# One-core Trainium2 kernel, linear attention, two mixtures of experts and a gated scan: late weights requested earlier, expert choice split over scan steps, state copies moved to ScalarE, last scan step in halves

## The chip, the cores and the metric

The kernel runs on one core of a Trainium2 chip. The metric is the device time of one execution in microseconds (us); three executions of the kernel before were timed, and one more was profiled.

## The reference, cut to what matters

The input is one sequence of 4096 rows of 256 numbers. All is float32.

```python
xn = layernorm(x)
x = x + chunk_attention(xn) + sum_e sigmoid(xn @ sel[e]) * (relu(xn @ keys[e]) @ values[e])   # 16 experts, dense
xn = layernorm(x)
g, v, d = (xn @ W[m] + b[m] for W, b in the three weights)        # m in 0..3
h[m] = scan over rows: h_t = a_t * h_(t-1) + sigmoid(g) * tanh(v),  a = 0.001 + 0.998 * sigmoid(d)
x = x + sum_m comb[:, m] * h[m]                                    # comb: softmax of the top 2 of 4 gates
      + w2[e] @ relu(w1[e] @ xn + b1[e]) + b2[e],  e = argmax of 8 # one expert for a row
```

## The kernel before, in words

Rows are worked in 8 groups of 512 rows (4 tiles of 128). Every float32 product is three matmuls of rounded parts (high x high, high x low, low x high, helper `mm3`, L374 on); so each operand has to be split in a high part (ScalarE) and a low part (VectorE) first.

**Stage A** (to about 522 us) does the attention and the dense experts of all groups. At its end SyncE's queue stores the gate mixture of the first 24 tiles (`mixture_store`, L525) and waits for that store (L693) before it goes on.

**Scan groups 0 to 3** (522 to 664 us). A group is 8 steps, step i for gate m = i // 2 and half c = i % 2 of the channels. TensorE makes three products of 512 columns (`scan_products`, L535) into three PSUM banks, ScalarE applies sigmoid, tanh and sigmoid and makes `a_b` (L1444), VectorE multiplies `xs_b` (L1697; GpSimd does it in group 0, L1549), scans (L1703), copies the last column to `hstate` (L1706), and multiplies by the mixture `comb_b` (L1714). From step 2 on the result is added to `accO` or `accT`, by GpSimd (`mix`, L1552) or by VectorE (L1723) where `mixed_on_dve(g)` holds: groups 2, 3 and 7. TensorE turns `accT` back to rows (`to_rows`, L1325) in step 2 of the next group as a rule. TensorE reuses a PSUM bank two steps later, ScalarE its output buffer two steps later. The six split weights of gates 2 and 3 (`WB_late`) come by six loads of 512 KB (`load_late`, L1180), the mixture of a group by a broadcast load of 1 MB (`load_comb`, L1159), the transposed rows of a group by two loads of 512 KB (`load_x1T`, L1150). For group 1 that load comes behind a wait (L1203) for the gate logits of the last group, which VectorE reads in group 0, step 5.

Within group 0, TensorE still turns and gates the last group's rows: it needs the low part `nT_l` (VectorE, L419, in front of step 3) for the gate matmuls (L459), whose result VectorE reads after step 5 (L435). Behind that, `choose_expert` (L1619) finds the expert of all 32 tiles in six operations on 128x256. The counts of rows per expert, the row positions and the table of expert slots follow in groups 1 and 2, and GpSimd scatters the rows to their experts' blocks.

**Experts** (664 to 903 us): 23 slots, of 256 rows or of 128 (every third). A slot is a first product (w1), relu and split, then a second product (w2). The halves of w1 and w2 are split ahead. In the first slot both ScalarE and VectorE split the second half of w2 (`w2_half(n, 1)`, L1492 and L1791) before they touch the first relu. SyncE's queue is one list written by hand: in `slot` (L1267) it waits until a half of w2 is split before it loads the next into its place, and behind that wait stand the biases b2, the rows, the small w1 and the bias b1 of the next slot (`load_b1`, L1244), which ScalarE's first relu of that slot needs.

**Scan groups 4 to 7** (903 us to the end). GpSimd gathers each row's expert result (`gather`, L1576) into `y_b` one group at a time, after the last use of the buffer, and gathers those of groups 0 to 2 between; GpSimd also adds the mixture in groups 4 to 6. In `total` (L1725) VectorE adds `y_b` to `x1_b` (L1735) and the turned scan result (L1744, for the last group L1741 in two pieces), and SyncE stores the sum before it loads the next `x1_b`. After the last step the chain is: xs, scan, copy, mixture, addition, four transposes (L1334), two sums (L1741), two stores (L1319).

```python
step(0, i)                      # VectorE, group 0 (L1813 to L1816)
if i == 5:
    gate_logits(dve, g)
    choose_expert()
```

## Time and profile before

| | |
|---|---|
| timed runs | 1053.69, 1055.35, 1055.56 us; median 1055.35 |
| the profiled execution | 1056.41 us, its span 1054.6 us |
| mean granted TensorE clock | 0.996 of full speed |
| TensorE (PE) busy | 1029.5 us, 98% |
| VectorE (DVE), ScalarE (ACT), GpSimd (POOL) busy | 753.7, 626.4, 366.9 us |

The span runs from the first to the last instruction; the remaining 1.8 us lie around it. In the rows, L with a number is a line of the kernel, the first number of a timeline row is the start in us from the span's start, the second the duration (of all the xN instructions that the row merges, from the first start to the last end), and square brackets give how long the engine sat idle just before and what ended that. SPq is SyncE's queue of DMA issues.

### The profile page before, as it was taken

How to read it: one execution, taken by the hardware profiler on the slowest of the kernel's cores; microseconds unless marked ns; L12 is line 12 of the kernel's file. 1: busy time of each engine (PE TensorE's matmuls, PEld its weight loads, DVE VectorE, ACT ScalarE, POOL GpSimd, SP SyncE). 2: the span in 40 equal slices, each digit the busy share in tenths (PEclk: the TensorE clock that was granted, in tenths of full speed). 3: DMA queues.
4: the chain of work that ended last, by engine and by line, in shares of the span. 5: the costliest groups of instructions: out<-in, count | busy, mean ns of one | idle time of the engine just before them, and what ended most of it. 6: DMA issues, size and time to landing. Idle time of an engine off the chain costs nothing. (4 is left out here: it accounts for less than half of the span.)

```text
span 1054.6 us, 19932 instructions
## 1 busy us (share of the span) xinstructions
PE 1029.5 (98%) x6564; PEld 920.0 (87%) x6564; DVE 753.7 (71%) x1264; ACT 626.4 (59%) x1138; POOL 366.9 (35%) x305
## 2 busy tenths in 40 slices
PE   6999999999999999999999999999999999999996
PEld 5898898989889898898877888899999999888885
DVE  4875756656575576767769879877777677488788
ACT  4553544444444454545565656788888888566664
POOL 2444453444444344343453783000000000264441
PEclk9999999999999999999999999999999999999998
DMA  5207111010111201513156266578877876332314
GB/s 162 91 17 239 41 40 60 0 64 35 40 60 40 85 15 40 181 61 140 41 202 259 93 214 243 199 241 264 273 264 249 276 249 210 126 125 100 116 58 139
DMA packets 74847, 141.07 MB, mean 134 GB/s; under 512 B 9904, under 2 KB 42544, under 8 KB 73776
## 3 DMA queue, kind: packets, MB, share of 16 engines
q1 hardware_dynamic: 65872, 126.94, 35.1%
q0 software_dynamic: 3072, 8.39, 2.4%
q10 hardware_dynamic: 5856, 5.15, 1.5%
q8 instruction: 25, 0.41, 0.2%
q14 instruction: 22, 0.18, 0.1%
HBM read 101.86 MB, written 38.60 MB: 133 GB/s over the span
## 5 line engine op out<-in xcount | busy, mean ns | idle before, releaser
L734 POOL TENSOR_TENSOR acc<-acc,ytmp 128x512 f32<-128x512 f32 x120 | 156.4, 1303 | 245.9 <-ACT ytmp L823 227.3
L1439 ACT ACTIVATE act_o<-ps,scan_bias 128x512 f32<-128x512 f32 x192 | 130.1, 688 | 106.5 <-PE ps L380 90.9
L823 ACT ACTIVATE ytmp<-ps,sel 128x256 f32<-128x256 f32 x256 | 107.6, 472 | 100.4 <-PE ps L1041 99.8
L889 DVE SCALAR_TENSOR_TENSOR hT_l<-ps,hT_h 128x512 fp32r<-128x512 f32 x128 | 87.7, 685 | 104.1 <-ACT hT_h L786 103.9
L1039 PE MATMUL ps<-vals_h,hT_h 128*128 128x256 f32 x512 | 145.2, 284 | 0.8 <-DVE hT_l L889 0.7
L1040 PE MATMUL ps<-vals_l,hT_h 128*128 128x256 f32 x512 | 143.6, 280 | 0.0
L1041 PE MATMUL ps<-vals_h,hT_l 128*128 128x256 f32 x512 | 143.5, 280 | 0.0
L786 ACT ACTIVATE hT_h<-ps 128x512 fp32r<-128x512 f32 x128 | 76.5, 598 | 96.1 <-PE ps L380 95.9
L1580 POOL DMA_INDIRECT y_b<-y_d,pos_i x20 | 25.6, 1280 | 290.0 <-DMA y_d<-y_sb 267.1
L925 DVE SCALAR_TENSOR_TENSOR acc<-ps,sel,acc 128x256 f32<-128x256 f32 x240 | 104.0, 474 | 3.0 <-PE ps L1041 2.9
L1703 DVE TENSOR_TENSOR_SCAN h_b<-a_b,hstate,xs_b 128x512 f32<-128x512 f32 x64 | 90.0, 1406 | 22.2 <-ACT a_b L1444 16.9
L378 PE MATMUL ps<-xT_h,keys_h 128*128 128x512 f32 x256 | 104.8, 409 | 0.7 <-DVE xT_l L419 0.7
L1039 PEld LDWEIGHTS ps<-vals_h,hT_h 128*128 128x128 f32 x512 | 96.3, 188 | 9.2 <-issue 2.5
L380 PE MATMUL ps<-xT_h,keys_l 128*128 128x512 f32 x256 | 101.1, 395 | 0.0
L379 PE MATMUL ps<-xT_l,keys_h 128*128 128x512 f32 x256 | 101.0, 394 | 0.0
L1040 PEld LDWEIGHTS ps<-vals_l,hT_h 128*128 128x128 f32 x512 | 96.2, 188 | 4.4
L1041 PEld LDWEIGHTS ps<-vals_h,hT_l 128*128 128x128 f32 x512 | 96.8, 189 | 0.0
L1412 PE MATMUL ps<-w_h,eT_h 128*128 128x256 f32 x312 | 90.2, 289 | 4.6 <-DVE eT_l L1765 4.0
L1413 PE MATMUL ps<-w_l,eT_h 128*128 128x256 f32 x312 | 87.9, 282 | 0.0
L1414 PE MATMUL ps<-w_h,eT_l 128*128 128x256 f32 x312 | 87.8, 281 | 0.0
L1765 DVE TENSOR_TENSOR eT_l<-t,eT_h 128x512 fp32r<-128x512 f32 (+1 forms) x92 | 55.7, 610 | 38.9 <-ACT eT_h L1488 38.7
L378 PE MATMUL ps<-x1T,WB_h 128*128 128x512 f32 (+1 forms) x192 | 76.4, 398 | 0.8 <-DMA x1T<-xT_d 0.8
(224 smaller groups left out, 2766.4 us busy)
## 6 DMA issues: line engine op xcount, KB each, us to landing
raw<-w SPq DMA_DIRECT2D x78, 512.0 KB, 5.1
x1T<-xT_d SPq DMA_DIRECT2D x16, 512.0 KB, 4.9
comb_b<-comb_d SPq DMA_DIRECT2D x8, 1024.0 KB, 8.5
w_small<-w SPq DMA_DIRECT2D x14, 512.0 KB, 4.5
xs_d<-zeros ACTq DMA_DIRECT2D x1, 4992.0 KB, 19.6
x_in<-x SPq DMA_DIRECT2D x8, 512.0 KB, 4.0
x_d<-x SPq DMA_DIRECT2D x8, 512.0 KB, 4.5
xn_d<-xn SPq DMA_DIRECT2D x8, 512.0 KB, 2.6
```

Source lines behind the costliest of these rows:

```text
L378: pe.matmul(dst, wh, xh, start=start, stop=False)
L379: pe.matmul(dst, wh, xl, start=False, stop=False)
L380: return pe.matmul(dst, wl, xh, start=False, stop=stop)
L734: pool.tensor_tensor(dst[:, 2:4, :], acc[:, 2:4, :], ytmp[:, k % 2, :, :], ALU.add).then_inc(acc23, 1)
L823: act.activation(ytmp[:, k % 2, j - 2, :], yb(k, j), ACT.Copy, scale=sel[:, j, k:k + 1]).then_inc(y_23, 1)
L925: dve.scalar_tensor_tensor(out=dst[:, j, :], in0=yb(k, j), scalar=sel[:, j, k:k + 1], in1=acc[:, j, :], op0=ALU.mult, op1=ALU.add).then_in ...
L1039: pe.matmul(yb(k, j), hT_h[:, k % 2, s], vals_h[:, k, :], start=True, stop=False)
L1040: pe.matmul(yb(k, j), hT_h[:, k % 2, s], vals_l[:, k, :], start=False, stop=False)
L1041: last_mm = pe.matmul(yb(k, j), hT_l[:, k % 2, s], vals_h[:, k, :], start=False, stop=True)
L1412: pe.matmul(dst, eT_h[:, j, t], w2_h[:, j, :], start=j == 0, stop=False)
L1439: act.activation(act_o[:, i % 2, w, :], ps[:, 3 * (i % 2) + w, :], func, bias=scan_bias[:, w, i:i + 1]).then_inc(act_g, 1)
L1703: dve.tensor_tensor_scan(h_b[:, i % 2, :], a_b[:, i % 2, :], xs_b[:, i % 2, :], hstate[:, i:i + 1], ALU.mult, ALU.add).then_inc(scan_ok, 1)
```

## The change

- SyncE's queue requests the six late weights as soon as the last low part of stage A is made, and stores the mixture behind them, not ahead.
- VectorE chooses the expert of the first 28 tiles after steps 1 and 2 of group 0, in two parts, and of the last 4 tiles after the gate logits.
- The eight scans of 32 that count rows per expert become one scan of 256, with a mask (`within`, made by GpSimd) that is zero at each expert's start.
- ScalarE copies the scan state of steps 0 to 5 (in its own step two later, ahead of `a_b`); VectorE keeps steps 6 and 7. In the last group there is no copy.
- In the first expert slot the second half of w2 is split after the second relu pair, on both engines.
- In groups 4 to 6 VectorE adds the mixture. GpSimd issues all 32 gathers one behind another, into buffers of their own; x1 of groups 4 to 7 is loaded ahead into `late_x`. The additions of y stand at fixed steps (`LATE_ADDS`), none in group 7.
- The last step (7, 7) runs in two halves of 256 columns on TensorE, ScalarE and VectorE; its second half is stored by ScalarE's queue.

```diff
-        return isinstance(g, int) and (2 <= g < B_FIRST or g == GROUPS - 1)
+        return isinstance(g, int) and g >= 2
...
-            sp.wait_ge(side_free, freed(GROUPS - 1, "lt") + 1)
-            mixture_store(sp, mix1)
-            sp.wait_ge(comb_st, 16)
             sp.wait_ge(acc_ip, GROUPS)
+            sp.wait_ge(h_lo, E0 * GROUPS)
...
-            sp.wait_ge(h_lo, E0 * GROUPS)
             for i in range(N_LATE):
                 load_late(i)
+            sp.wait_ge(side_free, freed(GROUPS - 1, "lt") + 1)
+            mixture_store(sp, mix1)
+            sp.wait_ge(comb_st, 16)
...
+            for g in range(B_FIRST, GROUPS):
+                sp.dma_start(late_x[:, g - B_FIRST], x1_d[g]).then_inc(late_x_in[g - B_FIRST], 16)
...
+            sp.wait_ge(fin_ok, GROUPS)
+            sp.dma_start(out_v[GROUPS - 1][:, 0:2, :], late_sum(GROUPS - 1)[:, 0:2, :]).then_inc(out_st, 16)
...
+            def last_products():
+                g, i = GROUPS - 1, MC - 1
+                m, c = divmod(i, DC)
+                s = slice(c * P, (c + 1) * P)
+                for half in (0, 1):
+                    pe.wait_ge(act_g, 3 * (MC * g + i - 1 + half))
+                    t = slice(half * HALF, (half + 1) * HALF)
+                    for w in range(3):
+                        for k in range(DC):
+                            last_mm = mm3(pe, ps[:, 3 * (1 - half) + w, t], WB_h[m][w][:, k, s], WB_l[m][w][:, k, s],
+                                          x1T[:, ring(g), 0, k, t], x1T[:, ring(g), 1, k, t], k == 0, k == DC - 1)
+                        last_mm.then_inc(b_full, 1)
+            def last_rows():
+                g = GROUPS - 1
+                pe.wait_ge(fin_ok, g)
+                pe.wait_ge(acc_ok, 6 * g + 5)
+                for j in range(JT):
+                    pe.transpose(side4[:, j, 0:P], accT[:, 0, j * P:(j + 1) * P], ident[:])
+                for half in (0, 1):
+                    pe.wait_ge(acc_ok, 6 * g + 6 + half)
+                    for j in (2 * half, 2 * half + 1):
+                        last_mm = pe.transpose(side4[:, j, P:2 * P], accT[:, 1, j * P:(j + 1) * P], ident[:])
+                    last_mm.then_inc(fin_full, 1)
             def to_rows(g):
...
+                if last_step(g, i):
+                    for half in (0, 1):
+                        t = slice(half * HALF, (half + 1) * HALF)
+                        for w, func in enumerate((ACT.Sigmoid, ACT.Tanh, ACT.Sigmoid)):
+                            act.wait_ge(b_full, 3 * (n + half) + w + 1)
+                            act.activation(act_o[:, i % 2, w, t], ps[:, 3 * (1 - half) + w, t], func,
+                                           bias=scan_bias[:, w, i:i + 1]).then_inc(act_g, 1)
+                        act.wait_ge(scan_ok, n - 1)
+                        act.wait_ge(act_g, 3 * (n + half) + 3)
+                        act.activation(a_b[:, i % 2, t], act_o[:, i % 2, 2, t], ACT.Copy, scale=0.998,
+                                       bias=0.001).then_inc(a_ok, 1)
+                    return
...
+                if i >= 2 and not final(g):
+                    act.activation(hstate[:, i - 2:i - 1], h_b[:, i % 2, GT - 1:GT], ACT.Copy).then_inc(hst_a, 1)
...
-                w2_half(n, 1)
+                if not zero(n):
+                    w2_half(n, 1)
                 for q in range(FJ // 2):
                     relu(n, q, st * P)
                     round_e(n, q, st * P)
+                    if zero(n) and q == 1:
+                        w2_half(n, 1)
...
+            act.wait_ge(fin_ok, GROUPS + 1)
+            act.dma_start(out_v[GROUPS - 1][:, 2:4, :], late_sum(GROUPS - 1)[:, 2:4, :]).then_inc(out_st, 16)
...
-                    if g >= B_FIRST and i == 4:
-                        pool.wait_ge(fin_ok, g)
-                        gather(y_b, pos_i[:, g * JT:(g + 1) * JT], y_in)
-                    if B_FIRST <= g < GROUPS - 1 and i == 5:
-                        f = g - B_FIRST
-                        gather(first_y[:, f], pos_i[:, f * JT:(f + 1) * JT], first_y_in[f])
...
-            for g in range(B_FIRST, GROUPS):
-                body(g)
+            for g in (3, 4, 0, 5, 6, 1, 2, 7):
+                index = pos_i[:, g * JT:(g + 1) * JT]
+                if g < B_FIRST - 1:
+                    gather(first_y[:, g], index, first_y_in[g])
+                else:
+                    gather(late_y[:, g - B_FIRST + 1], index, y_in[g - B_FIRST + 1])
...
+            def choose_expert(t0, t1, part):
+                n = t1 - t0
+                r = (P, n, E1)
+                some, best, marks = el[:, t0:t1, :], rmax[:, t0:t1], rt1[:, t0:t1, :]
+                if part == 0:
+                    if t0 == 0:
+                        dve.wait_ge(r_io, 7)
+                        dve.wait_ge(e_bias, 1)
+                    link(dve.tensor_tensor(some, logits[:, t0:t1, M:NL], ebias[:].unsqueeze(1).to_broadcast(r), ALU.add))
+                    link(dve.tensor_reduce(best, some, AX.X, ALU.max))
+                else:
+                    link(dve.tensor_tensor(marks, some, best.unsqueeze(2).to_broadcast(r), ALU.is_equal))
+                    link(dve.tensor_tensor(marks, marks, w8[:].unsqueeze(1).to_broadcast(r), ALU.mult))
+                    link(dve.tensor_reduce(best, marks, AX.X, ALU.max))
+                    dve.tensor_tensor(onehot[:, t0:t1, :], marks, best.unsqueeze(2).to_broadcast(r),
...
-                for e in range(E1):
-                    link(dve.tensor_tensor_scan(incl[:, e, :], ones[:, 0:TILES], tot[:, e, :], 0.0, ALU.mult, ALU.add))
+                link(dve.tensor_tensor_scan(incl[:].rearrange("p e t -> p (e t)"), within[:].rearrange("p e t -> p (e t)"),
+                                            tot[:].rearrange("p e t -> p (e t)"), 0.0, ALU.mult, ALU.add))
...
+            def last_half(half):
+                g, i = GROUPS - 1, MC - 1
+                n, b = MC * g + i, i % 2
+                t = slice(half * HALF, (half + 1) * HALF)
+                dve.wait_ge(act_g, 3 * (n + half) + 2)
+                dve.tensor_tensor(xs_b[:, b, t], act_o[:, b, 0, t], act_o[:, b, 1, t], ALU.mult).then_inc(xs_ok, 1)
+                dve.wait_ge(a_ok, n + half + 1)
+                dve.wait_ge(xs_ok, n + half + 1)
+                if half == 0:
+                    dve.wait_ge(hst_v, 2 * g)
+                    carry = hstate[:, i:i + 1]
+                else:
+                    dve.wait_ge(scan_ok, n + 1)
+                    carry = h_b[:, b, HALF - 1:HALF]
+                dve.tensor_tensor_scan(h_b[:, b, t], a_b[:, b, t], xs_b[:, b, t], carry, ALU.mult,
+                                       ALU.add).then_inc(scan_ok, 1)
+                dve.wait_ge(scan_ok, n + half + 1)
+                dve.wait_ge(acc_ok, 6 * g + i - 3)
+                dve.tensor_tensor(hw_b[:, b, t].rearrange("p (t q) -> p t q", q=P),
+                                  h_b[:, b, t].rearrange("p (t q) -> p t q", q=P),
+                                  comb_b[:, ring(g), 2 * half:2 * half + 2, M - 1, :], ALU.mult).then_inc(hw_ok, 1)
+                dve.wait_ge(fin_full, g)
+                dve.wait_ge(hw_ok, n + half + 1)
+                dve.tensor_tensor(accT[:, DC - 1, t], accO[:, DC - 1, t], hw_b[:, b, t], ALU.add).then_inc(acc_ok, 1)
...
+            def add_y(g):
+                if g < B_FIRST - 1:
+                    dve.wait_ge(first_y_in[g], 64)
+                    dve.tensor_tensor(first_res[g], first_res[g], first_y[:, g], ALU.add).then_inc(first_ok, 1)
+                    return
+                if g >= B_FIRST:
+                    dve.wait_ge(late_x_in[g - B_FIRST], 16)
+                dve.wait_ge(y_in[g - B_FIRST + 1], 64)
+                dve.tensor_tensor(late_sum(g), late_sum(g), late_y[:, g - B_FIRST + 1], ALU.add).then_inc(fin_sum, 1)
+            LATE_ADDS = {(4, 3): [3], (4, 6): [4], (5, 4): [0], (5, 5): [5], (5, 7): [6], (6, 4): [1], (6, 5): [2],
+                         (6, 7): [7]}
...
+                if i >= 2 and not final(g):
+                    dve.wait_ge(hst_a, (MC - 2) * g + i - 1)
...
-                dve.tensor_copy(hstate[:, i:i + 1], h_b[:, i % 2, GT - 1:GT]).then_inc(hst, 1)
+                if i >= MC - 2 and not final(g):
+                    dve.tensor_copy(hstate[:, i:i + 1], h_b[:, i % 2, GT - 1:GT]).then_inc(hst_v, 1)
...
-                dve.wait_ge(y_in, 64 * (g - B_FIRST + 2))
-                dve.tensor_tensor(x1_b[:], x1_b[:], y_b[:], ALU.add).then_inc(fin_sum, 1)
                 dve.wait_ge(fin_sum, g - B_FIRST + 2)
+                y = late_sum(g)
+                if g == GROUPS - 1:
+                    for half in (0, 1):
+                        j = slice(2 * half, 2 * half + 2)
+                        dve.wait_ge(fin_full, g + 1 + half)
+                        dve.tensor_tensor(y[:, j, :], side4[:, j, :], y[:, j, :], ALU.add).then_inc(fin_ok, 1)
+                    return
...
+                if i in (1, 2):
+                    choose_expert(0, TILES - JT, i - 1)
                 if i == 5:
                     gate_logits(dve, g)
-                    choose_expert()
+                    dve.wait_ge(side_free, post_use(GROUPS - 1, "lt")[2])
+                    for part in (0, 1):
+                        choose_expert(TILES - JT, TILES, part)
...
+                    for f in LATE_ADDS.get((g, i), []):
+                        add_y(f)
                     if i == rows_step(g) + 1:
                         total(g - 1)
-                    if g > B_FIRST and i == rows_step(g) + 2:
-                        f = g - B_FIRST - 1
-                        dve.wait_ge(first_y_in[f], 64)
-                        dve.tensor_tensor(first_res[f], first_res[f], first_y[:, f], ALU.add).then_inc(first_ok, 1)
```

Where the diff shows `LATE_ADDS` it is the table of the steps, group and step to the groups whose y is added there. `link` records one operation and waits for it. `w2_half` moves on VectorE as it does on ScalarE.

## Rows read from the trace of the kernel before

**Rows 1.** The page, busy time of an engine, share of the span, instructions

```profile
PE 1029.5 (98%) x6564; PEld 920.0 (87%) x6564; DVE 753.7 (71%) x1264; ACT 626.4 (59%) x1138; POOL 366.9 (35%) x305
```

**Rows 2.** The waits of TensorE: us in total, times, longest

```profile
PE ps L1334 <- DVE accT L1723: 4.5, 2, 2.8
PE ps L1412 <- DVE eT_l L1765: 4.0, 5, 2.4
PE ps L378 <- DMA x1T<-xT_d: 0.8, 1, 0.8
...
PE ps L459 <- DVE nT_l L419: 0.5, 1, 0.5
```

**Rows 3.** Windows, TensorE alone: stretch, its length, busy, granted clock, DMA share, GB/s

```profile
673.30:677.00 3.70, 3.70 (x18) 0.54 0.87 278
```

**Rows 4.** Timeline of the end, last two steps and last sums

```profile
1040.78 0.64 ACT L1444 ACTIVATE a_b<-act_o 128x512 f32<-128x512 f32 x1
...
1042.84 1.28 DVE L1703 TENSOR_TENSOR_SCAN h_b<-a_b,hstate,xs_b 128x512 f32<-128x512 f32 x1
...
1046.40 1.28 DVE L1703 TENSOR_TENSOR_SCAN h_b<-a_b,hstate,xs_b 128x512 f32<-128x512 f32 x1
...
1049.19 1.22 DVE L1735 TENSOR_TENSOR x_b<-x_b,y_b 128x1024 f32<-128x1024 f32 x1
1049.33 1.11 PE L1334 MATMUL ps<-ident,accT 128*128 128x128 f32 x4 [2.84 <-DVE accT L1723]
1050.55 1.29 DVE L1741 TENSOR_TENSOR x_b<-ps,x_b 128x512 f32<-128x512 f32 x2
1051.27 0.97 SPq L1319 DMA_DIRECT2D out<-x_b  x2
```

**Rows 5.** Groups of instructions: busy us, mean ns of one, idle before

```profile
L1706 DVE COPY hstate<-h_b 128x1 f32<-128x1 f32 x64 | 9.9, 154 | 2.2
L850 ACT ACTIVATE decay<-decay 128x1 f32<-128x1 f32 x1 | 0.2, 202 | 0.3 <-DMA decay<-log_decay 0.3
```

**Rows 6.** Timeline of group 0, and the landing times of all comb_b loads

```profile
519.80 0.69 DVE L889 SCALAR_TENSOR_TENSOR hT_l<-ps,hT_h 128x512 fp32r<-128x512 f32 x1 [0.82 <-ACT hT_h L786]
...
523.49 3.58 SPq L1182 DMA_DIRECT2D WB_late<-wl_d  x6
...
527.18 0.38 SPq L1164 DMA_DIRECT2D comb_b<-comb_d  x1
...
537.66 0.69 DVE L1714 TENSOR_TENSOR accO<-h_b,comb_b 128x512 f32<-128x512 f32 x1 [6.58 <-DMA comb_b<-comb_d]
...
543.37 1.22 DVE L419 TENSOR_TENSOR nT_l<-ps,nT_h 128x1024 fp32r<-128x1024 f32 x1
...
555.03 0.82 SPq L1156 DMA_DIRECT2D x1T<-xT_d  x2
...
DMA to landing us min/median/max: 4.4/8.5/10.5
```

**Rows 7.** Timeline, the first and the fourth operation of choose_expert

```profile
554.93 1.13 DVE L1624 TENSOR_TENSOR el<-logits,ebias 128x256 f32<-128x256 f32 x1
...
557.54 0.42 DVE L1628 TENSOR_TENSOR rt<-rt,w 128x256 f32<-128x256 f32 x1
```

**Rows 8.** Timeline of the first three expert slots

```profile
670.26 2.35 DVE L1759 TENSOR_TENSOR w_l<-raw,w_h 128x1024 fp32r<-128x1024 f32 x2
...
677.51 0.39 SPq L1247 DMA_DIRECT2D b1c<-b  x1
...
682.36 0.84 ACT L1480 ACTIVATE t<-ps,b1c 128x256 f32<-128x256 f32 x2 [0.51 <-DMA b1c<-b]
...
696.31 1.43 DVE L1765 TENSOR_TENSOR eT_l<-t,eT_h 128x256 fp32r<-128x256 f32 x4
```

**Rows 9.** Group 5: a window (PE, PEld, DVE, ACT, POOL busy), and its first scan

```profile
938.00:972.00 34.00, 34.00 (x151) 27.48 (x150) 29.42 (x35) 21.02 (x32) 18.02 (x14) 1.00 0.36 122
...
942.22 4.30 DVE L1703 TENSOR_TENSOR_SCAN h_b<-a_b,hstate,xs_b 128x512 f32<-128x512 f32 x1 [1.43 <-ACT a_b L1444]
```

More of the change, by code:

```diff
@@ L213, in build @@
     rmax = rr("rmax", [P, TILES], F32)
+    within = rr("within", [P, E1, TILES], F32)
     k256 = rr("k256", [P, 2, T // SLOT], F32)
@@ L594, in mixed_on_dve, with final, last_step @@
     def mixed_on_dve(g):
-        return isinstance(g, int) and (2 <= g < B_FIRST or g == GROUPS - 1)
+        return isinstance(g, int) and g >= 2
+    def final(g):
+        return isinstance(g, int) and g == GROUPS - 1
+    def last_step(g, i):
+        return isinstance(g, int) and (g, i) == (GROUPS - 1, MC - 1)
     def blocks(r, k):
@@ L1309, in _ @@
             sp.wait_ge(comb_st, 32)
-            with sp.Fori(B_FIRST, GROUPS - 1) as g:
-                body(g)
-            body(GROUPS - 1, True)
+            for g in range(B_FIRST, GROUPS):
+                sp.dma_start(late_x[:, g - B_FIRST], x1_d[g]).then_inc(late_x_in[g - B_FIRST], 16)
+            for g in range(B_FIRST, GROUPS):
+                body(g, g == GROUPS - 1)
             for g in range(B_FIRST - 1):
@@ L1315, in _ @@
                 sp.dma_start(out_v[g], first_res[g]).then_inc(first_st, 16)
-            for half in (0, 1):
-                sp.wait_ge(fin_ok, GROUPS + half)
-                tiles = slice(2 * half, 2 * half + 2)
-                sp.dma_start(out_v[GROUPS - 1][:, tiles, :], x1_b[:, tiles, :]).then_inc(out_st, 16)
+            sp.wait_ge(fin_ok, GROUPS)
+            sp.dma_start(out_v[GROUPS - 1][:, 0:2, :], late_sum(GROUPS - 1)[:, 0:2, :]).then_inc(out_st, 16)
             sp.wait_ge(first_st, 16 * (B_FIRST - 1))
@@ L1344, in body @@
                         pe.wait_ge(ys_ok, NSLOT)
+                    if last_step(g, i):
+                        last_products()
+                        continue
                     scan_products(pe, g, i)
@@ L1423, in _ @@
             every_slot(slot, pe)
-            with pe.Fori(B_FIRST, GROUPS) as g:
+            with pe.Fori(B_FIRST, GROUPS - 1) as g:
                 body(g)
-            to_rows(GROUPS - 1)
+            body(GROUPS - 1)
+            last_rows()
         @block.scalar
@@ L1526, in _ @@
             every_slot(slot, act)
-            with act.Fori(B_FIRST, GROUPS) as g:
+            with act.Fori(B_FIRST, GROUPS - 1) as g:
                 for i in range(MC):
                     step(g, i)
+            for i in range(MC):
+                step(GROUPS - 1, i)
+            act.wait_ge(fin_ok, GROUPS + 1)
+            act.dma_start(out_v[GROUPS - 1][:, 2:4, :], late_sum(GROUPS - 1)[:, 2:4, :]).then_inc(out_st, 16)
         @block.gpsimd
@@ L1542, in _ @@
                       allow_small_or_imprecise_dtypes=True).then_inc(r_io, 1)
+            pool.memset(within[:], 1.0).then_inc(r_io, 1)
+            pool.wait_ge(r_io, 6)
+            pool.memset(within[:, :, 0:1], 0.0).then_inc(r_io, 1)
             def xs(i):
@@ L1588, in body @@
                         xs(i + 1)
+                    if i >= DC and not mixed_on_dve(g):
+                        mix(g, i)
                     if isinstance(g, int) and (g, i) in SCATTER_AT:
                         scatter(SCATTER_AT.index((g, i)))
[L1591 to L1598 removed]
             rstd(pool, mv1, stats1[:, :, 0], rstd1, mvs1, pe1, rs1, GROUPS - 1)
@@ L1694, in step @@
                 m, c = divmod(i, DC)
+                if last_step(g, i):
+                    for half in (0, 1):
+                        last_half(half)
+                    return
                 if not zero(g):
@@ L1725, in total @@
             def total(g):
-                dve.wait_ge(x1b_in, 16 * (g + 1))
-                if isinstance(g, int) and g < B_FIRST - 1:
+                if g < B_FIRST:
+                    dve.wait_ge(x1b_in, 16 * (g + 1))
+                if g < B_FIRST - 1:
                     if zero(g):
@@ L1790, in slot @@
                     rows_out(*((r, k - 1) if k else (r - 1, ROUND - 1)))
-                w2_half(n, 1)
+                if not zero(n):
+                    w2_half(n, 1)
                 for q in range(FJ // 2):
                     low_e(n, q, st * P)
+                    if zero(n) and q == 1:
+                        w2_half(n, 1)
                     if q == 1 and not small(k) and bigs_left(r, k) > 0:
```

59 lines of the change are left out of this document (27 added, 32 removed).

## The prediction

> **What bounds the kernel now.** I read the page first: TensorE is busy for 98% of the span [rows 1], so an edit can win only where TensorE stands still or runs slow. The waits of TensorE list those places [rows 2]: 4.5 us ahead of the last transposes, 4.0 us in five waits for eT_l in the experts, 0.8 us for the x1T of group 1, 0.5 us for nT_l. That is 9.8 us that this change could reach. Windows over the experts then show one thing the waits hide: after the longest of the eT_l waits (2.4 us) the granted clock averaged 0.54 for 3.7 us [rows 3], that is, nearly all of the stretch went at 1.2 instead of 2.4 GHz, and some 1.7 us were lost with TensorE busy. Last, the timeline of the end: it is one chain through VectorE, from scan (7, 6) at 1042.84 to the last sum, which ends at 1050.55 + 1.29 = 1051.84 [rows 4]; behind it come only the stores.
>
> I call a difference within 0.2% (2.1 us) no change, for that is about what a measurement of this kernel can tell.
>
> **The end in halves.** Scan (7, 6) could start when a_b is ready, at 1040.78 + 0.64 = 1041.42 [rows 4], but starts 1.4 us later: VectorE is behind, because in steps 3 and 4 it does three additions of 1.22 us, of which the change leaves one in group 7. So I start scan (7, 6) at 1041.5. Scan, product and addition follow as before (1.28 + 0.7 + 0.7 + gaps of 0.15 = 2.8), to 1044.3. Then two halves, each xs, scan, product and addition of 256 columns. The price of 256 columns is 0.42 for a plain operation [rows 7]; a scan of 512 takes 1.28 [rows 4], so one of 256 takes between 0.64 and 0.8, say 0.7. With 0.15 of gaps a half is 0.42 + 0.7 + 0.42 + 0.42 + 0.15 = 2.1, two are 4.2, to 1048.5. ScalarE's halves come earlier than that, since its last whole a_b started 0.7 us after its own last sigmoid and VectorE is the late one. Of the four transposes (1.11 us) two are left behind the last addition, some 0.65; in their shadow VectorE sums the first half, and no addition of y (1.22, at 1049.19) stands there any more. The last sum of 0.65 ends at 1049.9, against 1051.84: **1.9 us less**. Bounds: if VectorE isn't caught up at (7, 6), 1.3 of it goes, and 0.6 is left; with no gaps it would be 2.4. The stores follow as before: ScalarE's queue is empty then, so I price its issue like one of SyncE's pair (0.97 for both). The Trainium skill (DMA: Bandwidth & Descriptors, Issuing engines are not separate DMA queues) says that DMAs from several engines share the same 16 DMA engines and that issuing from two saves only sequencer time; by it the second queue itself is worth at most half of 0.97, and none of that is in my sum; no row of the trace shows two queues at one output.
>
> **Late weights sooner.** SyncE can issue once the last low part is made, 519.80 + 0.69 = 520.5, not at 523.49 [rows 6]: 3.0 us sooner. No wait of TensorE for these weights is in rows 2, so this transfer was hidden and is worth nothing by itself. What matters is who is moved behind it. The mixture store and SyncE's wait for its landing now stand behind 3 MB. Before, from the first late issue to the landed comb_b it took 537.66 - 523.49 = 14.2 us for 4 MB. Now: six loads issued by 524.1 and moved by about 530 (3 MB at the rate of these 14.2 us is 10.6, less the ramp), the store just behind them, then comb_b, which takes 4.4 us with nothing ahead of it [rows 6]: it lands between 535.2 and 537.5. I take 535.5, as the DMA queue is then empty, 2.1 us sooner. Below nothing: up to 1 us later, if the store waits longer. The stores of x1 and xn1 go back with it in SyncE's list, but nothing reads them before group 1.
>
> **28 tiles in steps 1 and 2.** Six operations of 0.42 x 28/32 = 0.37 with gaps of 0.05 are 2.5 us, in front of nT_l. VectorE reaches them 2.1 us sooner by comb_b, and each step loses a copy (0.15 at most [rows 5]). So nT_l, at 543.37, moves by 2.5 - 2.1 - 0.3 = +0.1, and with it TensorE's 0.5 us wait. The logits are read after step 5, which ScalarE's a_b paces, so x1T is asked for at about 555.0 again and TensorE's 0.8 stays. The rest of choose_expert (5 us, from 554.93 to the scan at 559.9) leaves the path behind step 5, but no TensorE wait hung on it: cost and gain nothing. Group 0 together: **+0.1**, from -0.8 (both waits shrink) to +1.5.
>
> Rows 7 show that the price depends on GpSimd: the same kind of operation took 1.13 and 0.42. So each of the six may be up to 0.9 dearer where GpSimd's own products run, and its xs and mix of steps 2 and 3 do run there. The Trainium skill (SBUF — State Buffer, Who interferes with whom) says more: a VectorE operation with two SBUF inputs and a GpSimd operation that reads SBUF exclude each other, and the later one waits for the whole of the other. By that rule nT_l could come later by two whole GpSimd products, 2.6 us, and the sum would be +0.9 instead of -1.7; a scan that took 4.30 us, with GpSimd at work [rows 9], agrees with it. The rows alone give the third rival below.
>
> **State copies on ScalarE.** 42 copies of 0.20 [rows 5] are 8.4 us for an engine that is 59% busy; each stands ahead of a_b, which then comes 0.25 later. VectorE has been behind a_b nearly everywhere, so this costs nothing; where VectorE has caught up it costs 0.25 of slack against TensorE's 4.2 us a step. The one mask scan takes less than one of 512 (1.28) and replaces eight; TensorE has no wait in groups 1 to 3, so it is worth nothing either, and its mask (two small GpSimd operations) hides under GpSimd's idle time.
>
> **First expert slot.** TensorE waited 2.4 us because VectorE made both halves of w2 (2.35, from 670.26) before the first eT_l [rows 8]. Now one half (1.2) goes; with the copies VectorE starts some 0.5 sooner. TensorE starts 1.7 us sooner, then waits about 0.7 for the third eT_l, behind which w2 and w1 halves still stand. Without the long wait the clock should hold (+1.7). On its own: up to 2.7 us won by the end of this product. But SyncE's list waits for the second w2 half, which is now made 2 x 0.6 - 0.5 = 0.7 later, and behind that wait stand b2, rows, the small w1 and b1c. ScalarE already waited 0.51 for b1c, until 682.36 [rows 8]. From there ScalarE and VectorE run without a break until the eT_l at 696.31, on which TensorE waits again. So what the first slot wins, the second and third wait away: b1c lands where it did (the transfers ahead of it keep the queue full) or up to 0.7 later. **+0.1**, from -2.7 to +0.7, nearest to nothing because the row of 682.36 is a wait for the DMA and not for TensorE.
>
> **Groups 4 to 6.** VectorE takes 6 additions of 0.69 and one more of 1.22 per group, 5.4 us on top of 29.4 in the 34 us of group 5 [rows 9]; back come copies (0.9) and the stretch from GpSimd's products, which made one scan 4.30 where 1.28 is usual, 3.0 us. That leaves about 31 of 34 us, so TensorE does not wait. The 32 gathers cost GpSimd's time only. x1 comes 2 MB ahead, long before its use.
>
> **Sum.** -1.9 + 0.1 + 0.1 = -1.7. The profiled execution would go from 1056.41 to 1054.7; the median of the runs stands 1.06 below it, so 1055.35 - 1.7 = **1053.6**.
>
> **The rivals.** *The first slot's gain goes through.* If b1c comes in time, because the queue drains earlier by the 0.5 us that the first half is sooner, the clock's 1.7 of the 2.7 us stays: 1051.9. For it speaks that the clock loss was real; against it the 0.51 wait. *VectorE is not caught up at the end*: only 0.6 is won there, 1055.0; against it speaks that additions of 2.4 us go. *Slower: choose_expert blocks nT_l.* Place: the gate matmuls of group 0. If comb_b comes no sooner and GpSimd's products stretch the six operations by two times 0.9, nT_l is 2.5 + 1.8 = 4.3 later; TensorE loses that less the 0.8 of x1T: 1055.35 - 1.7 + 3.5 = 1057.2, and more if the clock falls as it did after 2.4 us of waiting. It decides from 2.5 us of delay on. *The change doesn't do what it says:* the late weights aren't late; that is in the forecast.
>
> **Chances.** Forecast 0.55 (own range 1052.6 to 1054.7; 0.18 of it beyond 0.2% faster), first rival 0.20, second 0.12 (all within 0.2%), slower rival 0.08, small losses that I miss 0.05. Faster by over 0.2%: 0.18 + 0.20 + 0.04 for an end near its bound of 2.4, so 0.42; slower 0.08; no change 0.50. The range takes in the first rival and reaches to 1055.7 upward, which leaves out most of the slower rival and the tip of the other: 1051.4 to 1055.7.
>
> **What would show it.** Right: the last sum's end 1.9 us nearer to the last TensorE product of group 7; comb_b's first use near 535.5; TensorE's eT_l wait in the first slot below 1.2 with the clock at 2.4 GHz, then new waits in slots two and three with ScalarE waiting for b1c until about 682.4. Wrong: nT_l past 545.5, TensorE waits in groups 4 to 6, no ScalarE wait for b1c, or scan (7, 6) more than 0.3 us behind its a_b.

## The result, and the profile after

The changed kernel takes 1059.28 us (median of 8 runs, 1058.14 to 1061.51), the kernel before 1055.28 beside it: a ratio of 1.0034, with a 95% interval of 1.0024 to 1.0045. It is slower by 4.0 us (3.6 by the ratio), where 1053.6 in 1051.4 to 1055.7 was forecast. The profiled execution took 1060.02 us with a span of 1058.3, against a span of 1054.6 before: 3.7 us more. Run once more in the third series below, the same kernel took 1076 us; that is told there.

The waits of TensorE, after (us in total, times, longest):

```profile
PE ps L464 <- DVE nT_l L424: 5.3, 1, 5.3
PE ps L1367 <- DVE accT L1791: 3.2, 2, 1.7
PE ps L1460 <- issue: 2.4, 2, 1.4
PE ps L1460 <- DVE eT_l L1892: 2.1, 5, 0.6
```

Against [rows 2], the wait for nT_l ahead of the gate matmuls has grown from 0.5 to 5.3 us. The wait at the end has shrunk, and that for x1T is gone, since TensorE now comes to it 7 us later. The waits for eT_l have shrunk from 4.0 to 2.1 us, but waits of the same products that the profile puts down to "issue" have grown from 0.6 to 2.4; together they are what they were, 4.6 and 4.5. Behind the wait the clock is low. Windows over TensorE alone, after (stretch, length, busy, granted clock, DMA share, GB/s):

```profile
546.00:549.00 3.00, 0.00 (x0) 0.86 0.00 0
549.00:556.00 7.00, 6.89 (x19) 0.57 0.37 150
```

TensorE stood still for all of the first window and worked through the second at a granted clock of 0.57, most of it at 1.2 instead of 2.4 GHz: the same as in [rows 3], but in another place. Its next mark, the transposes of the logits, comes 7.1 us later than before, that is 4.5 from nT_l and 2.6 from the clock. Marks further on complete the sum. The first product of the expert counts in group 1 comes 6.3 us later than before, since 0.8 of waiting for x1T is gone. The last transposes of rows in the experts come 5.5 later, the transposes of accT in group 7 also 5.5, and the last sum ends 3.7 later.

Why nT_l is late stands in two timelines. SyncE's queue, after:

```profile
520.47 3.04 SPq L1199 DMA_DIRECT2D WB_late<-wl_d  x6
523.55 0.45 SPq L531 DMA_DIRECT2D comb_d<-combT  x1
531.89 0.34 SPq L1182 DMA_DIRECT2D comb_b<-comb_d  x1
```

The late loads leave 3.0 us sooner, as the change wants [rows 6]. But the mixture store behind them, 48 KB, now takes 8.3 us to land (1.6 before, when nothing stood ahead of it); SyncE sits on that landing, and comb_b is asked for at 531.89, not at 527.18. VectorE, after:

```profile
538.39 0.69 DVE L1840 TENSOR_TENSOR accO<-h_b,comb_b 128x512 f32<-128x512 f32 x1 [7.79 <-DMA comb_b<-comb_d]
...
540.92 1.49 DVE L1698 TENSOR_TENSOR el<-logits,ebias 128x224 f32<-128x224 f32 x1
542.45 0.39 DVE L1699 TENSOR_REDUCE rmax<-el 128x28 f32<-128x224 f32 x1
542.87 1.28 DVE L1828 TENSOR_TENSOR_SCAN h_b<-a_b,hstate,xs_b 128x512 f32<-128x512 f32 x1
...
544.80 0.38 DVE L1701 TENSOR_TENSOR rt<-el,rmax 128x224 f32<-128x224 f32 x1
545.21 1.33 DVE L1703 TENSOR_TENSOR rt<-rt,w 128x224 f32<-128x224 f32 x1
546.58 0.39 DVE L1704 TENSOR_REDUCE rmax<-rt 128x28 f32<-128x224 f32 x1
547.00 0.92 DVE L1705 TENSOR_TENSOR onehot<-rt,rmax 128x224 f32<-128x224 f32 x1
547.84 1.21 DVE L424 TENSOR_TENSOR nT_l<-ps,nT_h 128x1024 fp32r<-128x1024 f32 x1
```

comb_b is used 0.7 us later than before (537.66), not 2.1 sooner, and the six operations of the choice sum to 4.9 us, not 2.2. Three of them, 1.49, 1.33 and 0.92 instead of 0.39, are stretched, and GpSimd's timeline shows beside what:

```profile
540.36 1.80 POOL L1622 TENSOR_TENSOR xs_b<-act_o 128x512 f32<-128x512 f32 x1 [5.08 <-ACT act_o L1500]
544.96 1.34 POOL L1634 TENSOR_TENSOR accO<-accO,hw_b 128x512 f32<-128x512 f32 x1 [2.80 <-DVE hw_b L1840]
546.26 1.41 POOL L1622 TENSOR_TENSOR xs_b<-act_o 128x512 f32<-128x512 f32 x1
```

GpSimd's operations end at 542.16, 546.30 and 547.67, the three of VectorE at 542.41, 546.54 and 547.92: each 0.25 behind, whenever it began. The reduction at 546.58, with one input, runs inside GpSimd's third operation and keeps its 0.39; the comparison at 544.80 began ahead of GpSimd's and keeps 0.38. The rule of the Trainium skill weighed in the prediction (SBUF — State Buffer, Who interferes with whom: a VectorE operation with two SBUF inputs and a GpSimd operation that reads SBUF exclude each other, the later waits for the whole of the other) fits these rows.

### The profile page after: what moved, and what is told of

Same layout as the page of the kernel before. It is cut to its first block and busy times, and to the rows that moved or that the text cites. A ratio compares the mean times of both kernels' runs of the same rounds, so it can differ in the third digit from the quotient of the medians.

```text
span 1058.3 us, 19899 instructions
## 1 busy us (share of the span) xinstructions
PE 1030.3 (97%) x6582; PEld 920.7 (87%) x6582; DVE 755.2 (71%) x1235; ACT 630.2 (60%) x1184; POOL 335.4 (32%) x289
## 5 line engine op out<-in xcount | busy, mean ns | idle before, releaser
L1653 POOL DMA_INDIRECT late_y<-y_d,pos_i x20 | 23.1, 1157 | 274.3 <-DMA y_d<-y_sb 268.5
L1828 DVE TENSOR_TENSOR_SCAN h_b<-a_b,hstate,xs_b 128x512 f32<-128x512 f32 x63 | 87.4, 1387 | 31.2 <-ACT a_b L1507 27.8
L385 PE MATMUL ps<-x1T,WB_late 128*128 128x512 f32 (+2 forms) x198 | 78.1, 395 | 0.0
```

The costliest lines, as they stand in the source:

```text
L385: return pe.matmul(dst, wl, xh, start=False, stop=stop)
```

## The experiments

Four series of four kernels and one of two, each beside the kernel before (1055.5 to 1055.8 in all of them).

**First series: which part holds nT_l up.** choose_back takes the choice away from steps 1 and 2:

```diff
-                if i in (1, 2):
-                    choose_expert(0, TILES - JT, i - 1)
...
-                        choose_expert(TILES - JT, TILES, part)
+                        choose_expert(0, TILES, part)
```

> The changed kernel, with the choice of the experts whole again behind step 5 of group 0 (32 tiles, one count); late loads, end in halves, copies and first slot stay changed. Theory A (the six operations ahead of nT_l hold TensorE up at the gate matmuls, and the stall then costs clock): nT_l starts at 543.8 instead of 547.84 (543.37 + 0.7 for the later comb_b - 0.3 for two copies gone), TensorE waits for it once for about 1.0 us instead of 5.30, the granted clock stays above 0.95 behind it, and the time is about 1054.3, that is 5 us less than the changed kernel's 1059.3. Rival B (the later comb_b, from the late loads asked for sooner, is what pushes nT_l): the time falls by less than 1.5 us, and nT_l stays past 546. Rival C (ScalarE's state copies and the additions of y mixed into groups 4 to 6 cost it): the stall goes, but the time stays above 1057.

Measured: 1055.49, ratio 1.0003 (0.9994 to 1.0012), so 3.8 us of the 4.0 are gone with it (3.3 of 3.6 by the ratios), though the time is 1.2 above the 1054.3 expected. VectorE and, under it, the window of TensorE:

```profile
538.82 0.69 DVE L1840 TENSOR_TENSOR accO<-h_b,comb_b 128x512 f32<-128x512 f32 x1 [7.96 <-DMA comb_b<-comb_d]
...
544.32 1.22 DVE L424 TENSOR_TENSOR nT_l<-ps,nT_h 128x1024 fp32r<-128x1024 f32 x1
```

```profile
547.00:556.00 9.00, 9.00 (x42) 1.00 0.23 93
```

comb_b is as late as in the change, but nT_l starts at 544.32, TensorE waits 1.5 us for it, and the clock holds. Rivals B and C fall.

loads_back restores SyncE's order (h_lo waited for and the six loads issued behind the landed mixture store):

```diff
+            sp.wait_ge(side_free, freed(GROUPS - 1, "lt") + 1)
+            mixture_store(sp, mix1)
+            sp.wait_ge(comb_st, 16)
             sp.wait_ge(acc_ip, GROUPS)
-            sp.wait_ge(h_lo, E0 * GROUPS)
...
+            sp.wait_ge(h_lo, E0 * GROUPS)
             for i in range(N_LATE):
                 load_late(i)
-            sp.wait_ge(side_free, freed(GROUPS - 1, "lt") + 1)
-            mixture_store(sp, mix1)
-            sp.wait_ge(comb_st, 16)
```

> The changed kernel, with the order of SyncE as before (mixture store and the wait for it ahead of the six late loads); the choice stays in steps 1 and 2. Theory A: comb_b lands 0.7 us sooner (first use 537.7), nT_l moves from 547.84 to about 547.1, TensorE still waits over 4 us for it, the clock still falls, and the time is 1058.4. Rival B: the stall falls under 2.5 us, the clock holds and the time is 1055 or less.

Measured: 1058.30, ratio 1.0027 (1.0018 to 1.0036). The rows of loads_back:

```profile
PE ps L464 <- DVE nT_l L424: 4.4, 1, 4.4
```

```profile
537.73 0.69 DVE L1840 TENSOR_TENSOR accO<-h_b,comb_b 128x512 f32<-128x512 f32 x1 [6.91 <-DMA comb_b<-comb_d]
```

```profile
547.00:556.00 9.00, 7.54 (x22) 0.63 0.29 117
```

The order of the loads is worth 0.7 us of comb_b and about 1 us of time; without the change in it, the choice still stalls TensorE and lowers the clock.

both_back has both edits, and shows what the rest of the change brings:

> The changed kernel with both undone: choice behind step 5, SyncE's order as before. What is left of the change is the end in halves, the copies on ScalarE, the first expert slot, the mask scan and the gathers. Theory A, with the forecast's terms (end -1.9, slots +0.1): nT_l at 543.1, TensorE's wait for it 0.3, time 1053.5, 1.8 us below the kernel before. Rival C: 1055 or more. If the first slot's gain goes through: 1051.9 or less.

Measured: 1054.45, ratio 0.9990 (0.9981 to 0.9999): 1.1 us faster than before, between the 1053.5 of theory A and the 1055 of rival C.

choose_gap is both_back with 28 tiles chosen inside step (0, 0), between its scan and the product that needs comb_b; the last 4 tiles stay behind step 5:

```diff
+                if zero(n):
+                    for part in (0, 1):
+                        choose_expert(0, TILES - JT, part)
                 if i == 0:
                     dve.wait_ge(comb_in, 16 * (g + 1))
```

> As the run with both undone, but 28 tiles are chosen right behind the first scan of group 0, while VectorE waits for comb_b anyhow (6.6 us before), and the last 4 tiles behind step 5. Theory A: the place of the six operations is what costs, not their number: they end by 536, ahead of comb_b at 537.7, nT_l stays at 543.1, and the time is that of the run with both undone within 0.5 us (the operations that leave step 5 were not on TensorE's path). Rival D (choosing in two portions costs by itself, wherever it stands): over 1 us more than with both undone.

Measured: 1053.91, ratio 0.9989 (0.9980 to 0.9998). VectorE in choose_gap:

```profile
530.92 1.31 DVE L1698 TENSOR_TENSOR el<-logits,ebias 128x224 f32<-128x224 f32 x1
...
533.96 0.39 DVE L1705 TENSOR_TENSOR onehot<-rt,rmax 128x224 f32<-128x224 f32 x1
537.54 0.69 DVE L1843 TENSOR_TENSOR accO<-h_b,comb_b 128x512 f32<-128x512 f32 x1 [3.19 <-DMA comb_b<-comb_d]
```

The six operations end at 534.35, with 3.2 us of the wait for comb_b left over. It is the place that costs, not the work, and rival D falls. Repeated in the fourth series as gap_again, the same kernel took 1053.68, ratio 0.9977 (0.9966 to 0.9988). It has the lowest median of all versions and was faster than the kernel before each time; from both_back, 0.5 us above it, it is not told apart.

**Second series.** before_choose adds to the kernel before the moved choice alone (choose_expert in two parts as in the change; TensorE waits for two counts of r_hot).

> The kernel before with one part of the change alone: 28 tiles chosen behind steps 1 and 2 of group 0, the last 4 behind step 5. Theory A: the same as taking it away shows from the other side (3.8 us, 1059.3 to 1055.5): comb_b is used at 537.7, the six operations take about 4.9 us, nT_l goes from 543.37 to 548.2, TensorE waits 5 us for it, the granted clock falls for about 7 us behind the wait, and the time is 1055.5 + 4.3 = 1059.8. The rival, that the choice only hurts together with the other parts: under 1057.

Measured: 1060.12, ratio 1.0050 (1.0037 to 1.0063); TensorE's wait for nT_l in it:

```profile
PE ps L459 <- DVE nT_l L419: 5.0, 1, 5.0
```

One part of the change, alone, makes 4.6 us. Its six operations sum to 3.8 us, not to the 4.9 expected, for here the product beside GpSimd's operation carries the stretch that the first of them carried in the change:

```profile
540.09 1.82 DVE L1720 TENSOR_TENSOR accO<-h_b,comb_b 128x512 f32<-128x512 f32 x1
541.84 0.38 DVE L1628 TENSOR_TENSOR el<-logits,ebias 128x224 f32<-128x224 f32 x1
```

The other three kernels of this series, and all four of the third, came out at 1075 to 1083 us.

**Third series: the same again.** To see whether the edits did that, the changed kernel itself was run once more, with the three beside it.

> The changed kernel once more, nothing edited. Three runs that stand between it and both_back came out 20 to 30 us slower on another chip (choose_14, gap_b1, halves_back), while the kernel before and before_choose kept their times there; in their traces TensorE, VectorE and ScalarE all stand still around 620 to 640 us and 940 to 965 us, where GpSimd issues indirect DMAs one behind the other. Theory F (the change itself brings this: from group 2 on GpSimd has no addition between its scatters and gathers, and on some chips the other engines are held up meanwhile): this run is at 1059.3 on a chip of the first kind and above 1075 on one of the other, and the other three of this call stand with it. Theory G (it comes from the edits of those three runs): 1059.3 here wherever it runs, and the three are slow again.

Measured: 1076.07, ratio 1.0221 (1.0181 to 1.0260), with the kernel before at 1055.66 beside it. So the edits are not to blame, as theory F has it; the same kernel had taken 1059.28, and 17 us depend on something outside of its text. That it is the chip, the other half of F, was wrong: this series ran on the chip of the first. TensorE and ScalarE in after_again:

```profile
617.34 0.48 PE L383 MATMUL ps<-x1T,WB_late 128*128 128x512 f32 x1
...
618.59 0.40 PE L385 MATMUL ps<-x1T,WB_late 128*128 128x512 f32 x1
```

```profile
617.46 0.63 ACT L1507 ACTIVATE a_b<-act_o 128x512 f32<-128x512 f32 x1
623.36 0.69 ACT L1500 ACTIVATE act_o<-ps,scan_bias 128x512 f32<-128x512 f32 x1 [5.26 <-PE ps L385]
626.15 0.69 ACT L1500 ACTIVATE act_o<-ps,scan_bias 128x512 f32<-128x512 f32 x1 [2.11 <-PE ps L385]
```

Six products fill the first bank by 619.0; ScalarE, idle since 618.1, reads it at 623.36, 4.4 us later, where it otherwise follows at once. The same happens around 950. Both stretches are those in which GpSimd issues its scatters and gathers one behind the other:

```profile
618.26 0.96 POOL L1646 DMA_INDIRECT xs_d<-xn_r,pos_i  x1 [0.30 <-issue]
619.53 0.96 POOL L1646 DMA_INDIRECT xs_d<-xn_r,pos_i  x1 [0.31 <-issue]
```

choose_14 leaves two operations of the choice behind step 1 and puts four behind step 4, with SyncE's order as before.

> SyncE's order as before, and the choice of 28 tiles split otherwise: its first two operations behind step 1 as in the change, the other four behind step 4, behind nT_l. Only 1.5 + 0.4 = 1.9 us stand ahead of nT_l, of which scan (0, 2), 2.32 us where GpSimd works beside it and 1.28 behind the choice, gives 1.0 back: nT_l at 544.2, TensorE waits 1.6 us, the clock holds, and the time is 1 us above the 1054.45 of both undone, 1055.4. If the clock falls after so short a wait too: 1057 or more.

> choose_14 again. Without those stalls the first expectation stands: nT_l about 0.8 us later than with both undone, TensorE waits 1.3 us (as in the first trace), the clock holds, 1055.4. With them: above 1070.

Measured: 1076.92 and 1075.51, with those stalls; group 0 lies ahead of them and can be read. TensorE waits 1.3 and 2.3 us for nT_l and the clock holds at 1.00 (547 to 558), but it waits 2.9 and 3.2 us for x1T: the operations behind step 4 now hold up step 5 and so the logits, and x1T is asked for at 557.22 and 558.01, not at 555.03 [rows 6]. What that costs in time can't be read under the stalls. So 28 tiles make TensorE wait wherever VectorE's step is on the path to nT_l or to the logits, and the gap ahead of comb_b was the free place.

gap_b1 is choose_gap with b1c asked for sooner in the first slot of a round:

```diff
                 load_b2(expert_at(r, k))
+                if k == 0 and left(r, k) > 0:
+                    load_b1(n + 1, expert_at(r, k + 1))
...
-                if left(r, k) > 0:
+                if k > 0 and left(r, k) > 0:
                     load_b1(n + 1, expert_at(r, k + 1))
```

> The run choose_gap (28 tiles chosen while VectorE waits for comb_b, SyncE's order as before) with one thing more: in the first slot of each round SyncE asks for b1c of the next slot ahead of the rows and the two halves of the small w1. Theory A (what the first slot wins is waited away for b1c, which stands behind those 1.25 MB): ScalarE's wait for b1c in the second slot goes from 3.9 us to under 1.5, its 0.5 to 1.3 us waits in the later rounds go, TensorE's stalls of 1.5 and 1.4 us in slots two and three shrink by 1.5 us or more together, and the time is 1053.9 - 1.5 = 1052.4. Rival (the whole DMA queue is full, another transfer takes its place as the last): 1053.9 within 0.5.

> gap_b1 again. Where the stalls of GpSimd's runs of indirect DMAs do not occur, theory A of its first run holds: ScalarE's wait for b1c in the second slot goes from 3.9 us to under 1.5 and the time is 1052.4 (1.5 below choose_gap); the rival is 1053.9. Where they occur: above 1070.

Measured: 1083.29 and 1079.41, worse than their neighbours. ScalarE's waits for transfers in gap_b1, and then in choose_gap:

```profile
ACT w_h L1524 <- DMA raw<-w: 16.7, 14, 2.0
ACT w_h L1517 <- DMA raw<-w: 13.5, 7, 2.8
ACT t L1545 <- DMA b1c<-b: 0.9, 5, 0.2
```

```profile
ACT w_h L1522 <- DMA raw<-w: 13.5, 13, 1.7
ACT t L1543 <- DMA b1c<-b: 9.7, 9, 3.9
```

The wait for b1c is gone (0.9 for 9.7), and waits for the raw weights, 16.7 us more, stand in its place: SyncE waits for the last relu of a slot before it may ask for b1c, and now the rows and weights stand behind that wait. From the transposes of rows in the first slot to those in the last, gap_b1 takes 225.7 us and gap_b1_again 227.9, the kernel before and choose_gap 218.2, and the other kernels with stalls 216.4 to 219.0; so this loss is the edit's and not the stalls'. It falls in the later rounds. In the first slots theory A held in part: from the first slot's transposes to the fifth's it takes 46.6 us, 47.9 in choose_gap and 47.5 in both_back. Over the whole the rival's mechanism held, another transfer is the last, at a higher price than it gave; its time of 1053.9 could not be put to the test.

halves_back is both_back with step (7, 7) whole (last_step is never true, last_rows gives way to to_rows, total waits for the whole fin_full); it was run three times.

> The run both_back with the last step whole again: products, sigmoids, scan, product, addition and transposes of step (7, 7) over 512 columns; the additions of y stay ahead in groups 4 to 6 and in group 7 none is left. Theory A as forecast (the halves overlap, and are where the 1.9 us come from): 1 us or more slower than both_back, 1055.5. Rival E, from the timelines of both_back and before: VectorE is the last engine either way and works 2.0 us for the halves' xs, scan, product and addition each, 3.35 us for the whole; what was won at the end is the additions of y taken out of group 7, and the halves are worth 0.3 us or less: 1054.7.

> halves_back again. Without those stalls: 1054.7 by rival E (the halves are worth 0.3 us, the additions taken out of group 7 the rest), 1055.5 by theory A (the halves are worth 1 us or more). With them: above 1070.

> halves_back a third time. The traces of the first two, whose end is undisturbed, have 7.0 and 7.2 us from the start of the last x1T product to the end of the last sum, both_back and choose_gap with the halves 5.9, the kernel before 8.1. So the halves should be worth 1.1 us after all (theory A, not rival E): both_back's 1054.45 + 1.0 = 1055.5. Rival E: 1054.7. If the stalls of 617 to 640 and 940 to 965 us occur: above 1070.

Measured: 1081.70 and 1079.42 with the stalls, and 1055.10, ratio 0.9999 (0.9990 to 1.0008), in the last series, without them. From the start of the last x1T product to the end of the last sum it takes 7.0, 7.2 and 7.25 us; with halves 5.9 in choose_gap and 5.8 in both_back (1043.39 to 1049.19); before 8.1. So the halves are worth 1.1 to 1.4 us there, and what left VectorE in group 7 (additions of y, copies) 0.8 to 1.1. By these rows rival E (0.3 us or less) falls; the medians, 0.65 apart with intervals that overlap, would not decide it.

**Fourth series: what opens the kernel to the stalls.** gap_again is the control. gap_copies_back puts the state copies back on VectorE, gap_mix_back the additions of groups 4 to 6 on GpSimd with the gathers between them, gap_copies_mix_back does both.

```diff
-                if i >= 2 and not final(g):
-                    act.activation(hstate[:, i - 2:i - 1], h_b[:, i % 2, GT - 1:GT], ACT.Copy).then_inc(hst_a, 1)
...
-                if i >= MC - 2 and not final(g):
+                if not final(g):
                     dve.tensor_copy(
```

```diff
-        return isinstance(g, int) and g >= 2
+        return isinstance(g, int) and (2 <= g < B_FIRST or g == GROUPS - 1)
...
+            GATHER_AT = {(4, 0): [3, 4], (4, 4): [0], (4, 6): [5], (5, 0): [6], (5, 4): [1], (5, 6): [2], (6, 0): [7]}
```

> The run choose_gap again, nothing edited, as the control of this series: 1053.9 where the stalls of 617 to 640 us and 940 to 965 us do not occur, above 1070 where they do.

> choose_gap with the state copies on VectorE again (64 less the 8 of group 7). Theory H (the stalls need ScalarE's copies, the only thing that differs from the kernel before in the stretch of 617 to 640 us): the control is above 1070 and this one at 1054 to 1055. If H is wrong: as the control. In a series without stalls: 1053.9 within 0.5, the copies are free on either engine.

> choose_gap with GpSimd adding the products of groups 4 to 6 again, its gathers spread between these additions. Theory I (the stalls come where indirect DMAs stand one behind the other for long): the stall of 940 to 965 us goes and that of 617 to 640 stays, the time is 10 to 12 us below the control. In a series without stalls: the time of the control, or up to 1 us more, because VectorE's scans beside GpSimd's additions are stretched (one took 4.30 instead of 1.28 us before).

> Both undone: copies on VectorE, additions of groups 4 to 6 on GpSimd. In a series with stalls, if either H or I or both together hold: 1054 to 1055.5. If it is above 1065, the stalls come from another part of the change. Without stalls: 1054 to 1055.

Measured: 1053.68, 1055.24 (ratio 0.9993), 1054.82 (0.9994) and 1055.00 (0.9991, 0.9982 to 1.0000); the control had no stalls, so H and I were not put to the test. Without stalls, each of the three is 1.1 to 1.6 us above the control, both edits together (1.3) no more than one. But choose_gap itself differs by 0.0012 in the ratio between its two series, nearly as much as these do from the control (0.0014 to 0.0017), so a gain from copies or additions is not shown. In a last series of two, copies_mix_again stood beside halves_third:

> gap_copies_mix_back again. If the stalls occur in halves_third beside it: 1055.0 if they need ScalarE's copies or GpSimd's unbroken gathers (theories H, I), above 1065 if not. If they do not occur: 1055.0 again.

Measured: 1054.32, ratio 0.9986 (0.9977 to 0.9995), again without stalls. Between 1055.00 and 1054.32 for one kernel lies what a median of a dozen runs leaves open here.

## Why the prediction was wrong, point by point

- **28 tiles in steps 1 and 2** is the step that failed. It said "Six operations of 0.42 x 28/32 = 0.37 with gaps of 0.05 are 2.5 us" and nT_l "+0.1". nT_l came 4.5 us later: comb_b 0.7, and from its use to nT_l 9.45 us instead of 5.71. The six operations cost 5.0 with their gaps, because three of them meet GpSimd's operations. One of the three stretches is not new: the product of step (0, 1), 1.81 us before, returns to 0.69, as the scan of choose_back does from 2.32 to 1.28. Two copies go besides. The price of [rows 7], 1.13 beside 0.42, was in front of me; I took the low value for all six and kept the high one for a rival.
- **Late weights sooner** failed in sign: comb_b at 535.5 was forecast, 538.39 measured: outside the 535.2 to 537.5 of the sum, 0.7 later than before, which only "up to 1 us later" allowed for. The 48 KB store behind 3 MB landed 8.3 us after its issue; I had let it follow at once, and had given comb_b 4.4 us from issue to landing, the least of [rows 6]; it needed about 6.4. By choose_back and both_back it is worth 1.0 us.
- **The slower rival** was what happened: its place (gate matmuls of group 0) and its trigger (comb_b no sooner, products of GpSimd) were right; 4.3 us for nT_l was forecast, 4.5 measured. That they are so close is in part luck, for it had comb_b unmoved and no stretch taken back. With the clock's fall the time was 1059.3 instead of 1057.2. It deserved far more than 0.08: its two conditions were not independent mishaps, and a row spoke for each. With 1.5 and 2.3 us of waiting the clock held, with 4.4 to 5.3 it fell; but it also fell after the 2.4 us in the expert slot of the kernel before [rows 3], so the length of the wait alone does not tell.
- **The end in halves** was right: forecast 1.9 us, measured 8.1 - 6.05 = 2.0 from the last product to the last sum's end (1049.52 to 1055.57 after), with VectorE caught up at (7, 6) as assumed: the scan starts at 1046.97, 0.04 behind its a_b, instead of 1.4. From its start to the end of the last sum it takes 8.6 us (8.35 in both_back) instead of 9.0. So the 1.3 and 0.6 of the forecast came as 1.4 and 0.4 to 0.65. In halves_third, with the whole step, the second stretch is 9.6: without the halves that part would have been a loss.
- **State copies, costed at nothing**: no wait shows for them; whether they bring a little is within the scatter of the fourth and fifth series.
- **The first expert slot** was right in its course. The wait for eT_l fell from 2.4 to 0.6 us and the clock held there (0.91 before, 1.00 after, from 672 to 690). ScalarE then waited 3.5 us for b1c:

```profile
688.83 0.84 ACT L1543 ACTIVATE t<-ps,b1c 128x256 f32<-128x256 f32 x2 [3.46 <-DMA b1c<-b]
```

  In both_back, where nothing has shifted, b1c is used at 682.59 against 682.36 [rows 8]. The transposes of rows in the second, third and fourth slot show the gain come and go, before and then both_back:

```profile
686.21 0.38 PE L1371 MATMUL ps<-ident,rows 128*128 128x128 f32 x2
695.60 0.60 PE L1371 MATMUL ps<-ident,rows 128*128 128x128 f32 x4
...
705.38 0.60 PE L1371 MATMUL ps<-ident,rows 128*128 128x128 f32 x4
```

```profile
683.22 0.38 PE L1419 MATMUL ps<-ident,rows 128*128 128x128 f32 x2
695.08 0.60 PE L1419 MATMUL ps<-ident,rows 128*128 128x128 f32 x4
705.63 0.60 PE L1419 MATMUL ps<-ident,rows 128*128 128x128 f32 x4
```

  3.0 us sooner, then 0.5, then 0.25 later, where both_back came to the slot 0.25 sooner. What gives the gain back are TensorE's waits of 1.3 and 0.6 us in the second slot and 1.4 in the third, where before there was only one of 0.6 in the third. The first rival fell. Over all slots the time from the first transposes of rows to the last is 0.8 to 0.9 us shorter in the change and both_back and not at all in choose_gap, inside the forecast's -2.7 to +0.7.
- **Groups 4 to 6**: VectorE is busy for 28.3 of 34 us (window 942 to 976 after), 31 was forecast. The forecast took back one stretched scan (3.0 us); a second scan (2.15 instead of 1.28) and an xs (1.05 instead of 0.68) were stretched too, and no more additions of y than before fell in the window, three in both. TensorE does not wait there, as said, while no stalls occur.
- **The sum**: with the two failed steps undone the rest gave 1054.45 (and 1053.91 with the choice in the gap), where 1053.5 was expected: 1.1 to 1.6 of the 1.8 us.

## What to carry to other kernels

Work that an engine does ahead of something awaited delays it, so put such work into a wait of that engine for something else (here VectorE's wait for comb_b) and not into the steps after it. A small store whose landing a queue waits for must not stand behind megabytes; count its landing with what is ahead. Price a two-input VectorE operation beside GpSimd's work at the end of GpSimd's operation, not at its own length, and where two rows each speak for a condition of the slower case, give that case its weight.

## What was not expected of the hardware

A stall of TensorE of 4.4 us or more at the gate matmuls cost time again by the clock: from the first gate matmul to the transposes of the logits it took 7.9 us in the change, 7.6 in loads_back, 6.8 in before_choose and 6.7 in after_again, against 5.25 before. So the price was 1.4 to 2.6 us for nearly the same stall.

Kernels with the change in them have a second level, some 20 us slower (1067.94 to 1088.17 us in all 39 runs of four such kernels, in two of six series), that never showed in 22 runs of the kernel before and 5 of before_choose in the same series. In it TensorE's finished products are taken up by ScalarE late (4.4 us in the rows above) while GpSimd issues indirect DMAs one behind the other. Neither an edit nor the chip alone explains it: the changed kernel was free of it in one series and full of it in another, and the chip of the first series showed it in the third. What the change adds to those stretches is ScalarE's copies and, in groups 4 to 6, gathers with no addition between them; whether it is one of these stays open, since the runs made for it fell into series without stalls.
